# Attention and expert kernel on one core: slot work spread over units, scatters and gathers issued by step

## The chip, the core and the metric

The kernel runs on one core of a Trainium2 chip. The metric is the device time of one execution in microseconds (us); lower is better. PE is the matrix engine (PEld its weight loads), DVE the vector engine, ACT the scalar engine, POOL GpSimd, and SP the engine that only issues DMAs and waits. The profile gives TensorE's granted clock as a share of full speed: 1.00 is 2.4 GHz and 0.50 is 1.2 GHz, the two levels between which it moves.

## What is computed

```python
xn = layernorm(x)                                   # x: (4, 1024, 128), fp32
q, k, v = xn @ Wq.T, xn @ Wk.T, xn @ Wv.T           # 16 heads of 8, rope on q and k
attn = softmax(causal(q @ k.T / sqrt(8))) @ v @ Wo.T
probs = softmax(xn @ router_w.T)                    # 4096 tokens, 8 experts
top_w, top_idx = top_k(probs, 2);  top_w /= sum(top_w) + 1e-9
ffn = sum over the 2 chosen of top_w * (relu(xn @ w1[e].T + b1[e]) @ w2[e].T + b2[e])
out = x + attn + ffn
```

## The kernel before

**Layout of the work.** There are four phases. A prologue normalises the rows, projects q, k and v with rope for the four sequences, writes the split parts of q and k to HBM (`parts_d`) and makes the router's logits. Then come 16 *units* (4 sequences x 4 groups of 4 heads). After the first two steps of unit 12 the *experts* run: 72 tiles of 128 slots each. Then the rest of unit 12 and units 13, 14 and 15, and the end: scaling, output projection and stores. `LAST` is 12.

**A unit has 12 steps**, one for each block of 128 keys in a half of 512 queries: steps 0 to 3 for the first half, steps 4 to 11 for the second. PE makes the scores of the step two further on (line 1271, `LEAD` is 2), ACT turns them into `probs` (line 764), POOL masks the diagonal block (line 660, steps 0 to 3 and 8 to 11), and PE multiplies with the values (line 1306). Beside it PE makes *items*, score pieces for later units (line 1237), and DVE takes their row maxima (lines 882 and 874). At step 6 DVE splits the next unit's maxima (lines 966 to 975), PE turns them (line 1260), at step 7 (`TURN`) DVE copies them to `mrow` (line 991), and SP stores them into the next unit's stack with four DMAs (line 418), for which the next unit's scores wait. `heads_out` (line 997) copies a half's result at steps 3 and 11. POOL's `stage_v` (line 649) prepares the next unit's values at step 3, which makes it a good mark of a unit's length.

**The slots.** Each token goes to two experts. DVE picks them (lines 930 to 947), PE counts tokens by two matmuls (`count_tokens`), and DVE works out each token's slots (`slot`, lines 1098 to 1118), which expert each tile belongs to (`expert`, lines 1121 to 1124) and the gates (lines 949 to 957). Each of these DVE steps waits for the one before. POOL *scatters* the normalised rows into `slots_in_d` in units 0 to 11 (line 634, 64 indirect DMAs) and *gathers* the experts' results from `slots_out_d` in units 12 to 15 (line 643, 64 indirect DMAs into 8 buffers, `GOT`); DVE adds each gathered block in `combine` (line 1029), and gather n waits for combine n - 8. The tables `SCATTERS` and `TRANSFERS` say how many POOL issues after each of a unit's 8 diagonal steps, `COMBINES` how many DVE adds at each of the 12 steps.

**What sets the order.** Each engine has one program, in the order written, and semaphores between engines; nothing is scheduled by a tool. `keep_warm` (line 1159) issues matmuls whose result nobody reads. POOL's part before unit 0 and before the rest of unit 12:

```python
            pool.wait_ge(s["slots_zeroed"], 16 * 4)
            pool.wait_ge(s["routed"], 1)
            pool.wait_ge(s["xn_ready"], B)
            all_units(pool, unit, None, before_last)   # before_last: waits for all 72 result stores
```

Since POOL does not take part in the experts, `before_last` stands ahead of unit 12's first mask.

Of the kernel before, what the change touches and what calls it, by code (L numbers as in the profile page):

```python
# [5 lines left out]
F32 = mybir.dt.float32  # L6
# [7 lines left out]
P = 128  # L14
# [11 lines left out]
PARTS = 2  # L26
# [96 lines left out]
def block_program(nc, x, w_projs, router, w_experts, b2, rope_t, consts, masks, out,  # L123
                  parts_d, zero_rows_d, heads_d, slots_in_d, slots_out_d, sums_d):
    ctx = ExitStack()
    with ctx:
# [51 lines left out]
        below = xnT[:, 0:TILES * E].rearrange("p (j e) -> p j e", e=E)  # L178
        ends = xnT[:, TILES * E:TILES * (E + 1)]
# [77 lines left out]
        zeros_ready slots_zeroed scattered """  # L257
# [57 lines left out]
        WARM = [30, 45, 1, 10, 22, 6]  # L315
# [7 lines left out]
        INVERTS = {4: 0, 5: 1, 7: 2}  # L323
# [6 lines left out]
        COMBINES = [[0, 0, 1, 0, 1, 2, 3, 3, 2, 1, 1, 1], [0, 1, 1, 0, 2, 2, 3, 3, 2, 1, 1, 1],  # L330
                    [0, 1, 1, 0, 2, 3, 3, 3, 2, 1, 1, 1], [1, 1, 1, 0, 1, 2, 2, 2, 2, 1, 1, 0]]
# [23 lines left out]
        def _(sp):  # L355
# [56 lines left out]
            def store_max_rows(u, par):  # L412

                sp.wait_ge(s["scores_read"], (u + 1) * MI)
                for g in range(2):
# [14 lines left out]
            def unit(u, r):  # L430
# [24 lines left out]
                if isinstance(u, int) and u == LAST + 3:  # L455
# [4 lines left out]
                    return  # L460
                store_heads(u, 1)
# [112 lines left out]
            store_max_rows(0, 0)  # L574
# [8 lines left out]
        def _(pool):  # L583
# [47 lines left out]
            def scatter(n):  # L631

                k2, t = divmod(n, NT)
                pool.indirect_dma_start(out=slots_in_d, out_offset=bass.IndirectOffsetOnAxis(  # L634
# [3 lines left out]
            def gather(n):  # L638

                t, k2 = gather_order(n)  # L640
                if n >= GOT:
# [11 lines left out]
            def unit(u, r):  # L653
                for n, (c, kb, q0) in enumerate(STEPS):
                    if kb >= 4 * c:
# [7 lines left out]
                        d = c * 4 + kb - 4 * c  # L663
                        if d == 3 and more(u, 1):
# [4 lines left out]
                        if u < LAST:  # L669
                            for i in share_of(SCATTERS, u, d):  # L670
                                scatter(i)
                        else:
                            for i in share_of(TRANSFERS, r, d):
                                gather(i)
# [7 lines left out]
            pool.wait_ge(s["slots_zeroed"], 16 * 4)  # L682
            pool.wait_ge(s["routed"], 1)
            pool.wait_ge(s["xn_ready"], B)
            all_units(pool, unit, None, before_last)
# [3 lines left out]
        def _(act):  # L689
# [104 lines left out]
            def experts():  # L794
                act.wait_ge(s["experts_loaded"], 16 * E)
                stage_w1(0, 0)
# [3 lines left out]
            for written in parts_written:  # L800
                act.wait_ge(written[1], 16 * PARTS * 2)
            unit(0)
# [11 lines left out]
        def _(dve):  # L814
# [134 lines left out]
            step(v.scalar_tensor_tensor(r_s[:, 0, :], share[:, 0, :], 1e-9, share[:, 1, :], ALU.add, ALU.add))  # L949
            step(v.reciprocal(r_s[:, 1, :], r_s[:, 0, :]))  # L950
            step(v.tensor_tensor(share[:], share[:], r_s[:, 1, :].unsqueeze(1).broadcast_to([P, 2, NT]), ALU.mult))
            step(v.tensor_tensor(gates[:], one1, wide(share[:, 0, :]), ALU.mult))
            step(v.tensor_tensor(m1, one2, wide(share[:, 1, :]), ALU.mult))
            v.tensor_tensor(gates[:], gates[:], m1, ALU.add).then_inc(s["chosen_ready"], 1)
            dve.wait_ge(s["logits_made"], B)
            dve.wait_ge(s["gT_made"], 1)
            v.tensor_copy(gT.rearrange("p a b -> p (a b)"), bank[:, 2, 0:2 * P]).then_inc(s["gT_kept"], 1)

# [40 lines left out]
            def unit(u, r):  # L999
                for j in range(NS):  # L1000
# [7 lines left out]
                    if j == TURN and more(u, 1):  # L1008
                        copy_rows(u + 1, (r + 1) % 4)
                    if isinstance(u, int) and u == UNITS - 1 and j == 6:  # L1010
# [71 lines left out]
            def experts():  # L1082
                dve.wait_ge(s["experts_loaded"], 16 * E)
                stage_w2(0, 0, expert_of(0))
                all_tiles(dve, tile)
                copy_y(TILES - 1, (TILES - 1) % 4)

            for n in range(sum(PREPARED.values()), NI):
# [5 lines left out]
            et = "p (e t) -> p e t"  # L1094
            earlier = bank[:, 3, 0:NT * E].rearrange("p (t e) -> p t e", e=E)
            inblock = bank[:, 3, NT * E:2 * NT * E].rearrange("p (t e) -> p e t", e=E)
            dve.wait_ge(s["counted"], 1)
            step(v.tensor_copy(total.rearrange(et, e=E), inblock))

            step(v.tensor_tensor_scan(upto, inner, total, 0.0, ALU.mult, ALU.add))  # L1100
            count = upto.rearrange(et, e=E)[:, :, NT - 1:NT].rearrange("p e o -> p (e o)")
            step(v.tensor_scalar(r_i[:, 0, :], count, float(ROUND - 1), None, ALU.add))
            bits = ROUND.bit_length() - 1
            step(v.tensor_scalar(r_i[:, 1, :], r_i[:, 0, :], bits, bits, ALU.logical_shift_right,
                                 ALU.logical_shift_left))
# [418 lines left out]
```

## Time and profile before

| | us |
|---|---|
| median of 3 runs | 768.5 (759.3 to 769.29) |
| the profiled execution | 764.56 |
| its span, first to last instruction | 762.8 |
| PE / DVE / ACT / POOL busy | 696.3 / 582.2 / 444.4 / 254.8 |
| mean granted clock | 0.955 |

The span begins at 0. The prologue ends at 107, units 0 to 11 and two steps of unit 12 end at 458, the experts run from 461 to 603, and the rest follows. PE counts as busy for 91% of the span, but its busy time includes stretches in which its matmuls take up to twice as long at the lower clock. Ends of matmuls are modelled, and a waiting engine is put down to what released it last; "remote" and "issue" mean that the trace names no releaser.

### The profile page before, as it was taken

The numbers are of one execution on the slowest core, as the hardware profiler recorded it, in microseconds if no ns is written. First come the engines' busy times: TensorE is split into PE (matmuls) and PEld (weight loads), VectorE is DVE, ScalarE is ACT, GpSimd is POOL, SyncE is SP. The second block draws the span as 40 slices with busy tenths as digits, with TensorE's granted clock in tenths as the row PEclk, the third lists the DMA queues.
The fourth block names the chain that finished last, engine by engine and source line by source line (L and its number), as shares of the span: only waits on it lengthen the run. The fifth ranks groups of instructions, "written<-read, shape, count | busy, mean of one in ns | idle before, by whom it ended". The sixth has DMA issues, their size and how long they took to land. (4 is left out here: it accounts for less than half of the span.)

```text
span 762.8 us, 18457 instructions
## 1 busy us (share of the span) xinstructions
PE 696.3 (91%) x6064; PEld 398.4 (52%) x6064; DVE 582.2 (76%) x1337; ACT 444.4 (58%) x962; POOL 254.8 (33%) x308
## 2 busy tenths in 40 slices
PE   8799898999999999999999997999999779788887
PEld 3456343434434444444444447999999624343434
DVE  6956978879879889889889884666666559797344
ACT  3455024666666677677677675666666346556541
POOL 2556212424334333433523520000000146565821
PEclk9999998999999999999999998999999869898989
DMA  8499950236355255134225413222222521111654
GB/s 222 129 231 231 236 100 20 45 78 102 73 116 100 60 96 80 38 54 79 50 45 77 63 32 95 78 69 69 69 69 69 135 52 38 46 34 40 162 126 130
DMA packets 64621, 69.36 MB, mean 91 GB/s; under 512 B 9934, under 2 KB 52430, under 8 KB 64490
## 3 DMA queue, kind: packets, MB, share of 16 engines
q1 hardware_dynamic: 60458, 60.08, 36.2%
q0 software_dynamic: 4096, 8.40, 4.2%
q8 instruction: 40, 0.66, 0.4%
q14 instruction: 27, 0.22, 0.1%
HBM read 41.11 MB, written 26.67 MB: 89 GB/s over the span
## 5 line engine op out<-in xcount | busy, mean ns | idle before, releaser
L764 ACT ACTIVATE probs<-bank 128x512 f32<-128x512 f32 (+2 forms) x640 | 314.8, 555 | 214.0 <-PE bank L1271 185.1
L882 DVE TENSOR_REDUCE mx<-bank 128x2 f32<-128x1024 f32 (+2 forms) x200 | 220.6, 1130 | 51.1 <-PE bank L1245 33.8
L1271 PE MATMUL bank<-stack 64*128 64x512 f32 (+3 forms) x768 | 196.4, 439 | 25.8 <-issue 16.0
L660 POOL TENSOR_SCALAR_AFFINE_SELECT probs<-probs 128x512 f32<-128x512 f32 x128 | 81.1, 635 | 406.7 <-ACT probs L764 253.6
L1306 PE MATMUL bank<-probs,vst 128*32 128x256 f32 (+2 forms) x2560 | 199.6, 387 | 5.0 <-POOL probs L660 5.0
L1271 PEld LDWEIGHTS bank<-stack 64*128 64x128 f32 x768 | 89.9, 189 | 157.5 <-issue 77.7
L1237 PE MATMUL bank<-stack 64*128 64x512 f32 (+3 forms) x768 | 149.2, 382 | 6.1 <-DVE mx L882 4.0
L874 DVE CUSTOM_DVE_ANT_0 q_high<-bank,later_s 128x384 bf16<-128x384 f32 (+1 forms) x240 | 135.1, 619 | 9.5 <-PE bank L1237 8.0
L1306 PEld LDWEIGHTS bank<-probs,vst 128*32 128x32 f32 x2560 | 52.2, 110 | 88.9 <-issue 72.7
L1237 PEld LDWEIGHTS bank<-stack 64*128 64x128 f32 x768 | 78.0, 193 | 39.1 <-issue 19.6
L1355 PE MATMUL bank<-tiles_s,staged 128*128 128x128 f32 x576 | 78.3, 280 | 0.7 <-ACT tiles_s L768 0.7
L1373 PE MATMUL bank<-staged,q_high 128*128 128x128 f32 x576 | 76.2, 275 | 0.5 <-DVE k_high L1062 0.5
L643 POOL DMA_INDIRECT k_high<-slots_out_d,slot x64 | 61.3, 958 | 40.6 <-DVE xn_all L1029 27.3
L1355 PEld LDWEIGHTS bank<-tiles_s,staged 128*128 128x128 f32 x576 | 71.4, 195 | 1.4 <-ACT tiles_s L768 1.4
L1373 PEld LDWEIGHTS bank<-staged,q_high 128*128 128x128 f32 x576 | 70.0, 192 | 0.7 <-issue 0.6
L778 ACT COPY staged<-early 128x516 f32 x72 | 44.8, 622 | 42.8 <-DVE q_high L1071 41.4
L634 POOL DMA_INDIRECT slots_in_d<-xn_all,slot x64 | 62.6, 977 | 12.8 <-issue 12.8
L1071 DVE TENSOR_SCALAR q_high<-bank,staged 128x128 f32<-128x128 f32 x144 | 43.9, 346 | 23.7 <-PE bank L1355 20.4
L789 ACT ACTIVATE q_high<-bank,staged 128x128 f32<-128x128 f32 x144 | 44.6, 360 | 1.6 <-PE bank L1373 1.1
L1062 DVE COPY k_high<-bank 128x128 f32<-128x128 f32 x72 | 21.0, 292 | 27.7 <-PE bank L1373 27.7
L997 DVE COPY xnT<-bank 128x512 f32<-128x512 f32 x32 | 22.0, 687 | 17.4 <-remote 10.3
L1159 PE MATMUL bank<-ones_b 128*128 128x512 bf16 x122 | 32.1, 415 | 1.1 <-POOL ones_b L586 1.1
(137 smaller groups left out, 477.4 us busy)
## 6 DMA issues: line engine op xcount, KB each, us to landing
stack<-parts_d SPq DMA_DIRECT2D x96, 128.0 KB
slots_in_d<-const_s SPq DMA_DIRECT2D x4, 1152.0 KB, 10.5
tiles_s<-slots_in_d SPq DMA_DIRECT2D x72, 64.0 KB, 1.8
slots_out_d<-k_high SPq DMA_DIRECT2D x72, 64.0 KB, 1.6
early<-in_w_experts SPq DMA_DIRECT2D x8, 514.0 KB
stack<-parts_d SPq DMA_DIRECT2D x64, 64.0 KB
parts_d<-probs SPq DMA_DIRECT2D x8, 512.0 KB, 6.1
heads_d<-xnT SPq DMA_DIRECT2D x124, 18.0 KB
```

What stands on the lines that cost most here:

```text
L634: pool.indirect_dma_start(out=slots_in_d, out_offset=bass.IndirectOffsetOnAxis(ap=slot[:, k2, t:t + 1], axis=0), in_=xn_all[:, t, :], in_o ...
L643: pool.indirect_dma_start(out=got[n % GOT], out_offset=None, in_=slots_out_d, in_offset=bass.IndirectOffsetOnAxis(ap=slot[:, k2, t:t + 1], ...
L660: pool.affine_select(out=t, in_=t, compare_op=ALU.is_ge, fill=0.0, base=0, pattern=[[0, HG], [1, P]], channel_multiplier=-1).then_inc(s["d ...
L764: nc.scalar.activation(to, src, ACT.Exp, scale=SCALE).then_inc(s["probs_made"], 1)
L778: nc.scalar.copy(w_s[r % 2][:, 0:F + FC], early[:, bass.ds(e * WIDE, F + FC)]).then_inc(s["w1_staged"], 1)
L874: last = v.tensor_tensor_reduce(hidden_scores[n % 2 * 2 + g][:, 0:w], ms[(r * MI + n) % 2][:, g * HALF:g * HALF + w], later_s[:, HALF - w: ...
L882: v.tensor_reduce(to, src.rearrange("p g (a k) -> p g a k", k=w), AX_X, ALU.max, negate=True).then_inc(s["scores_read"], 1)
L1237: last = mm(at[:, col:col + w], qstk[r][g][:, hp, qb * P:(qb + 1) * P], kstk[r][g][:, hp, c * HALF:c * HALF + w], start=not both or i == 0 ...
L1271: made = mm(st_of(u, n, i)[:, col:col + HALF - q0], kstk[r][g][:, hp, kb * P:(kb + 1) * P], qstk[r][g][:, hp, c * HALF + q0:(c + 1) * HALF ...
L1306: last = mm(pv[32 * h:32 * h + 32, begin:end], vst[r % 2][:, kb, h, :], probs[n % 3][:, h, begin:end], start=kb == 0 and begin == 0, stop= ...
L1355: last = mm(at[:, col:col + P], w_s[r % 2][:, f * P:(f + 1) * P], xtT[r % 2], start=True, stop=True)
L1373: last = mm(pv[:, 0:C], hid[r % 2][:, f * P:(f + 1) * P], w_s[r % 2][:, F + FC + f * C:F + FC + (f + 1) * C], start=f == 0, stop=f == FC - 1)
```

## The change

The slot chain of the prologue is cut up: only the two counts are copied out of PSUM there, and the rest runs on DVE in units 0 to 3 at the end of steps 7, 8 and 9 (`rank`). The gates are made in unit 2 and turned by PE at the start of the experts. POOL issues scatters and gathers by a table with one entry for each of 12 steps, and waits at steps without a mask for that step's `probs`; scatters start in unit 2. The wait for the result stores moves to the first gather (step 3 of unit 12). SP loads the first four expert tiles in unit 11. ACT issues two of the four stores of the first unit's maxima. `keep_warm` calls are shortened before and added between the first scores and ahead of the experts. The inversions of the head sums in unit 13 move from steps 4, 5 and 7 to 8, 9 and 10.

```diff
-        WARM = [30, 45, 1, 10, 22, 6]
+        WARM = [30, 35, 1, 10, 12, 6]
-        INVERTS = {4: 0, 5: 1, 7: 2}
+        INVERTS = {8: 0, 9: 1, 10: 2}
-        SCATTERS = [[1, 0, 0, 3, 1, 0, 0, 1]] * 4 + [[1, 0, 0, 2, 1, 0, 0, 1]] * 8
+        SCATTERS = ([[0] * 12] * 2 + [[0, 0, 0, 1, 1, 1, 1, 1, 1, 0, 0, 1]] * 4 + [[0, 0, 0, 1, 1, 1, 1, 1, 0, 0, 0, 1]] * 5
+                    + [[0, 0, 1, 1, 1, 1, 1, 1, 0, 0, 0, 0]])
-        TRANSFERS = [[1, 0, 0, 11, 2, 1, 0, 2]] * 2 + [[1, 0, 0, 12, 2, 1, 0, 2]] + [[1, 0, 0, 9, 2, 0, 0, 0]]
+        TRANSFERS = [[0, 0, 0, 2, 2, 2, 2, 2, 2, 1, 1, 2], [1, 0, 0, 2, 2, 2, 2, 2, 2, 1, 1, 2],
+                     [1, 0, 0, 2, 2, 2, 2, 2, 2, 1, 1, 2], [1, 1, 1, 2, 2, 2, 2, 2, 1, 0, 0, 0]]
...
 # SP, in unit(u, r), after the maxima of the next unit are stored
+                if isinstance(u, int) and u == LAST - 1:
+                    sp.wait_ge(s["scattered"], 16 * 2 * NT)
+                    for j in range(4):
+                        load_tile(j, j)
                 store_heads(u, 1)
             def experts():
-                sp.wait_ge(s["scattered"], 16 * 2 * NT)
-                for j in range(4):
-                    load_tile(j, j)
                 all_tiles(sp, tile)
...
-            store_max_rows(0, 0)
+            store_max_rows(0, 0, range(1))
...
 # POOL
             def gather(n):
+                if n == 0:
+                    for r in range(4):
+                        pool.wait_ge(y_stored[r], 16 * TILES // 4)
...
+                    else:
+                        pool.wait_ge(s["probs_made"], banks_before(u, n + 1))
+                    if u < LAST:
+                        for i in share_of(SCATTERS, u, n):
+                            scatter(i)
+                    else:
+                        for i in share_of(TRANSFERS, r, n):
+                            gather(i)
-            def before_last():
-                for r in range(4):
-                    pool.wait_ge(y_stored[r], 16 * TILES // 4)
...
 # ACT, before unit 0
+            act.wait_ge(s["scores_read"], MI)
+            for n in range(2):
+                act.dma_start(qstk[0][1][KROWS + n:KROWS + n + 1, :, :] ..., mrow[0] ...).then_inc(mrow_stored[0], 16)
...
 # DVE: the gates (lines 949 to 957) leave the prologue; the slot chain becomes these functions, called in unit(u, r)
+            v.tensor_copy(place, earlier).then_inc(s["counts_kept"], 1)
+            v.tensor_copy(total.rearrange(et, e=E), inblock).then_inc(s["counts_kept"], 1)
+            def rank(u, j):
+                if (u, j) == (0, TURN):
+                    first_slots()        # was lines 1100 to 1106
+                if (u, j) == (0, TURN + 1):
+                    next_slots()         # 1107 to 1109
+                if (u, j) == (0, TURN + 2):
+                    places()             # 1110 to 1114
+                if (u, j) == (1, TURN):
+                    slots_of(0)          # 1116 to 1118
+                if (u, j) == (1, TURN + 2):
+                    slots_of(1)          # the same, then "routed"
+                if (u, j) == (2, TURN):
+                    share_out()          # 949 to 951
+                if (u, j) == (2, TURN + 2):
+                    gates_out()          # 952 to 954
+                if (u, j) == (3, TURN):
+                    expert_tiles()       # 1121
+                if (u, j) == (3, TURN + 2):
+                    expert_ends()        # 1123, 1124, then "expert_known"
 # DVE, in experts(), after stage_w2
+                dve.wait_ge(s["gT_made"], 1)
+                v.tensor_copy(gT ..., bank[:, 2, 0:2 * P]).then_inc(s["gT_kept"], 1)
...
 # PE
             pe.wait_ge(mrow_stored[0], mrow_count(0, 0))
-            pe.wait_ge(s["gT_kept"], 1)
+            pe.wait_ge(s["scores_read"], MI + AT_START)
             for n in range(LEAD):
                 for h in range(HG):
                     score(0, 0, n, h)
+                    if n or h:
+                        keep_warm(1, 7)
-            pe.wait_ge(s["routed"], 1)
+            pe.wait_ge(s["counts_kept"], 2)
...
                 turn_tile(0, 0)
+                turn_gates()             # waits for probs of unit 12, steps 0 and 1; two transposes
+                keep_warm(3, 7)
                 all_tiles(pe, tile)
```

DVE at the end of the prologue, from the copy of the first unit's maxima to the first maxima of unit 1's items. Before:

```order
L991 COPY mrow<-bank 64x128
L1098 COPY staged<-bank 128x256
L1100 SCALAR_TENSOR_TENSOR staged<-const_s,staged 128x256
L1102 TENSOR_SCALAR r_i<-staged 128x8
L1104 TENSOR_SCALAR r_i<-r_i 128x8
L1106 CAST r_e<-r_i 128x8
L1107 MEMSET r_e 128x8
L1108 SCALAR_TENSOR_TENSOR r_e<-r_e 128x8
L1109 TENSOR_TENSOR r_e<-r_e 128x8
L1110 TENSOR_TENSOR staged<-staged 128x256
L1111 TENSOR_TENSOR staged<-staged,r_e 128x256
L1114 TENSOR_TENSOR staged<-bank,staged 128x256
```

Nine more rows follow (lines 1116 to 1124) before the maxima of line 882. Now, where line 893 is the old 882 and 992 the old 991:

```order
L967 TENSOR_TENSOR mx<-mx 128x4x4
L972 CAST mneg<-mx 128x16 x2
L976 TENSOR_TENSOR mneg<-mx,mneg 128x16 x2
L992 COPY mrow<-bank 64x128
L1104 COPY staged<-bank 128x256
L1105 COPY staged<-bank 128x256
L893 TENSOR_REDUCE mx<-bank 128x2x2 x4
```

Two copies stand where 21 instructions stood; the rest is in units 0 to 3.

POOL from step 8 of unit 11 into unit 12, with what each waits for. Before:

```order
L634 DMA slots_in_d<-xn_all,slot 9216x128
L660 AFFINE_SELECT probs<-probs 128x4x128 [waits y_stored3,probs_made,y_stored2,y_stored0,y_stored1]
L643 DMA k_high<-slots_out_d,slot 128x128
L660 AFFINE_SELECT probs<-probs 128x4x128 [waits probs_made] x3
L649 COPY vst<-v_all 128x32x8 [waits probs_used]
L643 DMA k_high<-slots_out_d,slot 128x128 x7
L643 DMA k_high<-slots_out_d,slot 128x128 [waits combined] x4
```

Now (line 670 is the old 660, 659 the old 649, 653 the old 643):

```order
L670 AFFINE_SELECT probs<-probs 128x4x128 [waits probs_made] x8
L659 COPY vst<-v_all 128x32x8 [waits probs_used]
L653 DMA k_high<-slots_out_d,slot 128x128 [waits y_stored2,y_stored3,y_stored1,y_stored0]
L653 DMA k_high<-slots_out_d,slot 128x128
L653 DMA k_high<-slots_out_d,slot 128x128 [waits probs_made]
...
L653 DMA k_high<-slots_out_d,slot 128x128 [waits combined,probs_made]
L653 DMA k_high<-slots_out_d,slot 128x128 [waits combined]
```

The wait for the result stores stands behind unit 12's first four masks, and every second gather waits for the `probs` of its step.

PE at the start of the experts. Before:

```order
L1271 MATMUL bank<-stack 128x384 x2
L1237 MATMUL bank<-stack 128x384 x2
L1364 MATMUL bank<-const_s,tiles_s 128x128
L1355 MATMUL bank<-tiles_s,staged 128x128 x4
```

Now (1423 is the old 1364, 1414 the old 1355, 1278 the turning of the gates, 1214 `keep_warm`):

```order
L1330 MATMUL bank<-stack 128x384 x2
L1296 MATMUL bank<-stack 128x384 x2
L1423 MATMUL bank<-const_s,tiles_s 128x128
L1278 MATMUL bank<-const_s,logits 128x128 x2
L1214 MATMUL bank<-ones_b 128x512 x3
L1414 MATMUL bank<-tiles_s,staged 128x128 x4
```

The gates are turned between the first tile's turn and its first product.

## Rows read from the trace of the kernel before

**Rows 1.** Windows over chosen stretches: busy us of each engine, granted clock, DMA

```profile
core 0: us, PE busy (x) PEld busy (x) DVE busy (x) ACT busy (x) POOL busy (x), PEclk, DMA share, GB/s
151.20:240.40 89.20, 83.25 (x823) 37.20 (x819) 74.05 (x157) 59.05 (x120) 33.70 (x47) 0.96 0.46 89
268.00:295.70 27.70, 26.83 (x280) 12.15 (x273) 24.62 (x53) 19.64 (x40) 10.27 (x15) 1.00 0.44 74
612.10:650.10 38.00, 32.16 (x279) 13.66 (x283) 29.06 (x68) 19.69 (x40) 21.69 (x28) 0.86 0.19 44
650.10:685.90 35.80, 29.41 (x278) 13.16 (x281) 31.48 (x75) 20.12 (x40) 21.71 (x28) 0.90 0.15 39
685.90:719.00 33.10, 27.07 (x237) 11.75 (x237) 20.50 (x46) 19.90 (x40) 22.08 (x27) 0.90 0.31 76
```

**Rows 2.** Timeline, end of the prologue: start, length, engine, line, names [idle before]

```profile
85.91 0.42 DVE L947 TENSOR_TENSOR staged<-staged 128x256 bf16<-128x256 f32 x1
88.52 0.44 PE L1219 MATMUL bank<-const_s,logits 128*128 128x128 f32 x2 [0.46 <-DVE logits L954]
89.60 10.27 DVE L882 TENSOR_REDUCE mx<-bank 128x2 f32<-128x1024 f32 x9
101.46 2.50 SPq L418 DMA_DIRECT2D stack<-mrow  x4
101.98 4.92 PE L1159 MATMUL bank<-ones_b 128*128 128x512 bf16 x22
106.83 0.73 PE L1271 MATMUL bank<-stack 64*128 64x512 f32 x3
109.46 0.69 DVE L882 TENSOR_REDUCE mx<-bank 128x4 f32<-128x512 f32 x1 [0.25 <-DVE expert L1124]
```

**Rows 3.** Windows: steps 0 to 3 of units 0 and 1, and of unit 12

```profile
112.20:122.60 10.40, 10.40 (x72) 4.31 (x71) 7.38 (x21) 3.05 (x8) 4.79 (x7) 0.58 0.22 45
138.90:145.70 6.80, 6.61 (x85) 3.27 (x82) 5.49 (x11) 3.67 (x9) 2.25 (x3) 1.00 0.06 17
605.60:615.80 10.20, 8.62 (x56) 3.06 (x58) 5.07 (x15) 1.75 (x4) 6.32 (x9) 0.50 0.73 111
```

**Rows 4.** Timeline, start and end of the experts

```profile
461.03 0.45 PE L1364 MATMUL bank<-const_s,tiles_s 128*128 128x128 f32 x1 [3.49 <-DMA tiles_s<-slots_in_d]
461.83 2.08 PE L1355 MATMUL bank<-tiles_s,staged 128*128 128x128 f32 x8 [0.35 <-ACT tiles_s L768]
468.90 1.06 PE L1355 MATMUL bank<-tiles_s,staged 128*128 128x128 f32 x8
606.41 0.62 POOL L660 TENSOR_SCALAR_AFFINE_SELECT probs<-probs 128x512 f32<-128x512 f32 x1 [151.98 <-DMA slots_out_d<-k_high]
607.18 1.08 PE L1306 MATMUL bank<-probs,vst 128*32 128x256 f32 x8 [3.21 <-POOL probs L660]
```

**Rows 5.** Timeline, POOL's run of eight gathers in unit 12, ACT and PE beside it

```profile
612.67 0.98 POOL L643 DMA_INDIRECT k_high<-slots_out_d,slot  x1 [0.16 <-issue]
...
621.29 1.08 ACT L764 ACTIVATE probs<-bank 128x512 f32<-128x512 f32 x2 [3.03 <-remote]
621.45 0.94 POOL L643 DMA_INDIRECT k_high<-slots_out_d,slot  x1 [0.30 <-issue]
621.94 0.49 PE L1271 MATMUL bank<-stack 64*128 64x512 f32 x1 [3.13 <-issue]
```

**Rows 6.** The same view: ACT in unit 15's run of gathers, the last of four

```profile
729.91 1.09 ACT L764 ACTIVATE probs<-bank 128x512 f32<-128x512 f32 x2 [3.14 <-remote]
```

**Rows 7.** Lines view, unit 13: DVE's adds and inversions, mean ns

```profile
L1029 DVE SCALAR_TENSOR_TENSOR xn_all<-k_high,share,xn_all 128x128 f32<-128x128 f32 x17 | 6.0, 383 | 0.0
L1035 DVE RECIPROCAL tiles_s<-tiles_s 128x128 f32<-128x128 f32 x3 | 2.8, 943 | 0.0
```

**Rows 8.** Timeline, the last gathers and the add that waits

```profile
743.87 0.94 POOL L643 DMA_INDIRECT k_high<-slots_out_d,slot  x1 [0.15 <-issue]
750.64 0.35 DVE L1029 SCALAR_TENSOR_TENSOR xn_all<-k_high,share,xn_all 128x128 f32<-128x128 f32 x1 [8.00 <-DMA k_high<-slots_out_d,slot]
```

More of the change, by code:

```diff
@@ L177, in block_program @@
         rt2 = [staged[:, 1, i * NT * E:(i + 1) * NT * E] for i in range(4)]
-        below = xnT[:, 0:TILES * E].rearrange("p (j e) -> p j e", e=E)
-        ends = xnT[:, TILES * E:TILES * (E + 1)]
+        below = staged[:, 0, 0:TILES * E].rearrange("p (j e) -> p j e", e=E)
+        ends = staged[:, 0, TILES * E:TILES * (E + 1)]
         gates = logits
@@ L410, in load_stacks, with store_max_rows @@
                                  ).then_inc(stack_loaded[r], 16)
-            def store_max_rows(u, par):
+            def store_max_rows(u, par, halves=range(2)):
                 sp.wait_ge(s["scores_read"], (u + 1) * MI)
-                for g in range(2):
+                for g in halves:
                     for n in range(2):
@@ L662, in unit @@
                                            ).then_inc(s["diag_masked"], 1)
-                        d = c * 4 + kb - 4 * c
-                        if d == 3 and more(u, 1):
+                        if n == 3 and more(u, 1):
                             if past(u):
@@ new lines, in next_slots, with places @@
+            def next_slots():
+                step(v.memset(r_e[:, 3, :], 1.0))
+                step(v.tensor_tensor_scan(r_e[:, 1, :], r_e[:, 3, :], r_e[:, 0, :], 0.0, ALU.mult, ALU.add))
+                step(v.tensor_tensor(r_e[:, 2, :], r_e[:, 1, :], r_e[:, 0, :], ALU.subtract))
+            def places():
+                step(v.tensor_tensor(upto, upto, total, ALU.subtract))
+                step(v.tensor_tensor(upto.rearrange(et, e=E), upto.rearrange(et, e=E),
+                                     r_e[:, 2, :].unsqueeze(2).broadcast_to([P, E, NT]), ALU.add))
+                step(v.tensor_tensor(place, place, upto.rearrange("p (e t) -> p t e", e=E), ALU.add))
@@ L1117, in _, with slots_of @@
+            def slots_of(n):
+                step(v.tensor_tensor(m0, (one1, one2)[n], place, ALU.mult))
                 step(v.reduce_sum(r_s[:, n, :], m0, AX_X))
                 step(v.tensor_copy(slot[:, n, :], r_s[:, n, :]))
-            dve.wait_ge(s["v_made"], B)
-            step(v.tensor_tensor(below, r_e[:, 1, :].unsqueeze(1).broadcast_to([P, TILES, E]),
-                                 starts.unsqueeze(2).broadcast_to([P, TILES, E]), ALU.is_le))
-            step(v.reduce_sum(ends, below, AX_X))
@@ L1124, in _, with share_out @@
-            step(v.tensor_scalar(expert[:], ends, float(E - 1), None, ALU.min))
-            dve.sem_inc(s["routed"], 1)
-            dve.wait_ge(parts_written[0][0], 16 * PARTS * 2)
-            dve.wait_ge(s["later_ready"], 1)
+                if n:
+                    dve.sem_inc(s["routed"], 1)
+            def share_out():
+                step(v.scalar_tensor_tensor(r_s[:, 2, :], share[:, 0, :], 1e-9, share[:, 1, :], ALU.add, ALU.add))
+                step(v.reciprocal(r_s[:, 3, :], r_s[:, 2, :]))
+                step(v.tensor_tensor(share[:], share[:], r_s[:, 3, :].unsqueeze(1).broadcast_to([P, 2, NT]), ALU.mult))
@@ new lines, in gates_out, with expert_tiles @@
+            def gates_out():
+                step(v.tensor_tensor(gates[:], one1, wide(share[:, 0, :]), ALU.mult))
+                step(v.tensor_tensor(m1, one2, wide(share[:, 1, :]), ALU.mult))
+                v.tensor_tensor(gates[:], gates[:], m1, ALU.add).then_inc(s["chosen_ready"], 1)
+            def expert_tiles():
+                dve.wait_ge(s["chosen_ready"], 2)
+                step(v.tensor_tensor(below, r_e[:, 1, :].unsqueeze(1).broadcast_to([P, TILES, E]),
+                                     starts.unsqueeze(2).broadcast_to([P, TILES, E]), ALU.is_le))
@@ new lines, in expert_ends @@
+            def expert_ends():
+                step(v.reduce_sum(ends, below, AX_X))
+                step(v.tensor_scalar(expert[:], ends, float(E - 1), None, ALU.min))
+                dve.sem_inc(s["expert_known"], 1)
+            def rank(u, j):
[17 more added lines that the diff above has]
+                    expert_ends()
```

69 lines of the change are left out of this document (29 added, 40 removed).

## The prediction

> **What bounds the kernel now.** I read the windows by stage first, with one unit to a row, because the busy shares of the whole span mix stages with different limits. A unit in the middle of the run takes 27.7 us, in which PE is busy for 26.8 and DVE for 24.6, at a full clock: PE bounds it, and DVE has 3.1 us to spare [rows 1]. Units 1 to 3, from one `stage_v` to the next, take 89.2 us together, 6.1 more than three times 27.7, with the same busy DVE and ACT and a clock of 0.96. What differs there is POOL: its table lets it issue three scatters in a row, where later units have two. Units 12, 13 and 14 take 38.0, 35.8 and 33.1 at clocks of 0.86 and 0.90, with DVE busy for 29.1, 31.5 and 20.5 and PE for 27.1 in the third [rows 1]. So no engine is full there; 19.3 us are waiting (106.9 less 29.1, 31.5 and 27.1).
>
> Then I read the timeline at the places where a stretch is longer than its engines' work. At the end of the prologue the first scores, at 106.83, stand behind 22 warming matmuls, which stand behind nothing but the engine's own order, while the maxima are stored by four DMAs of SP [rows 2]. Steps 0 to 3 of unit 0 and of unit 12 take 10.4 and 10.2 us at clocks of 0.58 and 0.50; the same steps of unit 1 take 6.8 at 1.00 [rows 3]. The experts begin after 3.49 us of an idle PE and end with 3.21 [rows 4]. In a run of eight gathers ACT and PE are idle for 3.03 and 3.13 us at the same moment, with no releaser in the trace; the last of four such places shows 3.14 [rows 5, 6].
>
> **The change part by part.** The sum is made against the profiled execution, 764.56, which lies 3.9 below the median of 768.5.
>
> *First scores, −4.3.* DVE's picked experts are ready at 86.33, and its first maximum starts at 89.60, behind the gates and the transposes of PE at 88.52 [rows 2]. Without both, and with ten warming matmuls fewer (0.22 each, 4.92 by 22), PE counts at 86.4 (two matmuls, 0.4), makes the first pieces, and DVE reads them 0.7 after: 87.45, 2.15 sooner. The rest of the chain moves along, and SP begins the stores at 99.3. Two stores on SP take 1.25 of the 2.50 for four; ACT issues the others beside it. Twelve warming matmuls take 2.7 and end at 102.5 instead of 106.90, and the scores start there, if the stores have landed: −4.3. The trace bounds the landing: the four stores had ended issuing at 103.96 and PE went on at 106.83, so at most 2.9 later. That gives 103.5 at worst, −3.3.
>
> *Head of unit 0, −2.5.* It takes 3.6 more than that of unit 1 [rows 3]. Two things go: DVE, busy with the slot chain until 109.2, reads unit 1's pieces again at 109.46 [rows 2], and PE idles or waits in between; now the chain is two copies, and PE is kept active by warming matmuls between the first scores. Both ends are open: nothing returns if the clock falls all the same (0), all of it if not (3.6). I take two thirds.
>
> *Units 1 to 3, −6.1, and the moved work, +1.* Scatters now come one to a step, from unit 2 on. The trace has no such spacing; the nearest row is the unit with two in a row, 27.7. The moved chain lies between 101.5 and 109.2, 7.7 us [rows 2], and the gates add 2.15: some 9.8 us of DVE in four units, at steps 7 to 9, where DVE's queue also holds the maxima copied for the next unit. Four times the 3.1 us of spare DVE are 12.4, so that cover is there, and I take 1 for what falls at a bad moment. If the cover were gone, all 9.8 would show. Unit 0 and unit 1 have no scatters at all; that they must catch up later costs nothing by count, since no unit issues more than seven where it was six.
>
> *Start of the experts, −3.* PE's 3.49 us go if the tiles lie there already [rows 4]. Behind them the first tile's products took 2.08 us instead of 1.06, at the lower clock; with the next tile's that is at most some 1.5 more, if PE is not idle long enough to lose its clock. Against it stand two transposes (0.44), three warming matmuls (0.7) and ACT's and DVE's staging of the weights, which is next late: PE had been idle for about as long as they worked. Bounds −1.5 and −4.5, value −3. What SP does in unit 11 (a wait for the 64 scatters, the last at step 7, ahead of the loads and the head stores) sits at the end of that unit, and nothing waits on SP there before unit 12.
>
> *End of the experts, −6.* The mask at 606.41 waited for the last result stores, and PE for the mask: 3.21 [rows 4]. With the wait behind unit 12's four masks, 3.1 goes. The head of unit 12 then ran 3.4 us longer than at full clock [rows 3]; if PE does not idle, most of this goes too: −2.9. The bounds are −3.1 and −6.5.
>
> *Gathers in units 12 to 14, −7.* The 19.3 us of waiting, less 1.3 that lie in the head of unit 12 after its `stage_v` and are counted there, leave 18.0. Some of it is the run of eight to twelve gathers at one step. The change spaces them, but not far: two at each of steps 3 to 8, each 1.25 us from start to start [rows 5], are 2.5 us of issuing in a step of 2.3 us (27.7 by 12). POOL still issues nearly back to back through half of the unit. Moreover DVE's adds, 0.38 each, and the three inversions of 0.94 [rows 7] stay, with unit 13 bound by DVE at 31.5. All of it would be −18, none of it 0; I take −7, nearer to none, because the row nearest to the new spacing is the run itself.
>
> *Unit 15 and the end, −0.5.* DVE's add at 750.64 came 6.8 us after the gather at 743.87 was issued, and it was idle for 8.00 us [rows 8]; the last gather is still at step 8.
>
> Sum: −4.3 −2.5 −6.1 +1 −3 −6 −7 −0.5 = −28.4, so 736.2 for an execution like the profiled one, and with half of its distance to the median **738**.
>
> **The rivals.** *The gathers cost what they cost, spaced or not: 745.* The idle places at the runs [rows 5, 6] are brief beside 18 us, and the lower clock of these units may come from PE's share in them. Then the −7 is 0. For it: the nearly unbroken issuing. Against: units with two scatters in a row show none of it.
> The Trainium skill bears on this (SBUF — State Buffer, "SBUF: two separate sides"): PE, ACT and DVE's own pair of ports never wait on anyone, and engine ports and DMA ports are disjoint. By that rule the spacing changes nothing and the time is that of this rival; but rows 5 show PE and ACT idle together at a run of gathers, so the trace does not quite agree.
>
> *The stalls vanish: 727.* If the 3 us places and the clock both come from runs longer than two, the term is −18 and the time 11 less than forecast.
>
> *New waits eat it: 758.* Adds now follow their gathers by one step. A loaded gather took 6.8 us [rows 8], three steps; eight buffers hold the queue, but if DVE waits 0.5 us at each of the 24 steps with two adds, that is 12 us, and an uncovered slot chain adds 8: 738 + 20.
> For an unloaded gather the Trainium skill (DMA: Bandwidth & Descriptors, "Anatomy of one DMA — SWDGE (gpsimd) path") gives about 2.0 us and the bytes over 436e3; my estimate from it is 2.15 for 64 KB, within a step, and by it this rival costs nothing. The 6.8 of the trace is measured with other traffic.
>
> *Slower than before: 785.* The clock stays at its lower level in units 12 to 15, because PE waits a little at every step instead of much at one. Its price is the ratio of the heads, 10.4 to 6.8, or 1.53 [rows 3], on the stretch that now takes about 140: four units of 42 are 169, +29. With 12 us of waits this is 41, and the 7 of the gathers are not gained: 738 + 48, about 785. [...]
>
> **How the numbers follow.** The forecast, 738 with its own bounds from 729 to 748, gets 0.55; spacing without effect 0.18; the vanished stalls 0.12; new waits 0.10; slower 0.05. That the change does not do what it says is small and inside these. The range must leave out no more than 2 in 10: from 722, below the case at 727, to 758, that of the new waits. Two per cent of 768.5 is 15.4, about what a measurement of this kernel can tell from no change; the limits are 753.1 and 783.9. The forecast, both cases of the gathers and a little of the new waits lie below 753: 0.83 faster, 0.13 same, 0.04 slower.
>
> **What would show it.** First scores near 102.5; steps 0 to 3 of unit 0 in 7 to 8 us at full clock; units 1 to 3 at 28 each, with the slot work in DVE's idle places; PE idle below 1 us at the start of the experts, and none before the first product of unit 12; units 12 to 14 at 34, 34 and 30. I am wrong if PE still shows places of 3 us beside spaced gathers, if DVE waits for `k_high` at the steps after, or if the clock in units 1 to 3 stays below 1.00 without runs of scatters.

## The result, and the profile after

The changed kernel takes 744.8 us (median of four runs, 741.8 to 749.1) against 768.9 (759.3 to 769.4). The ratio is 0.972, with a 95% interval from 0.964 to 0.980: faster. The forecast was 738, with a range of 722 to 758. The profiled execution has a span of 740.8 us, 22.0 less than the one before, and a mean granted clock of 0.965.

The windows over the stretches that [rows 1] shows for the kernel before, then unit 13's values staged to the end as one stretch, and the first probabilities to the values of unit 2:

```profile
core 0: us, PE busy (x) PEld busy (x) DVE busy (x) ACT busy (x) POOL busy (x), PEclk, DMA share, GB/s
149.10:233.90 84.80, 80.95 (x823) 36.89 (x819) 78.05 (x172) 58.76 (x120) 31.05 (x43) 1.00 0.49 89
261.70:289.30 27.60, 26.73 (x277) 12.17 (x273) 24.54 (x53) 19.60 (x40) 12.19 (x18) 1.00 0.43 80
596.80:629.00 32.20, 29.81 (x275) 13.18 (x273) 27.75 (x66) 19.91 (x40) 22.18 (x27) 0.89 0.35 65
629.00:667.30 38.30, 32.48 (x273) 13.88 (x265) 32.01 (x76) 19.60 (x40) 21.77 (x28) 0.84 0.15 38
596.80:740.80 144.00, 125.05 (x1027) 58.28 (x1023) 101.60 (x212) 73.14 (x148) 82.64 (x96) 0.89 0.36 86
105.20:149.10 43.90, 40.92 (x356) 17.99 (x356) 35.57 (x87) 25.59 (x52) 8.55 (x14) 0.92 0.20 31
```

The three units that had runs of three scatters now take 84.8 where they took 89.2, at a clock of 1.00 instead of 0.96. The middle unit is as it was. The unit after the first gathers takes 32.2 instead of 38.0, but the next one 38.3 instead of 35.8. The same two long stretches before read so:

```profile
612.10:762.80 150.70, 123.18 (x1033) 57.25 (x1033) 100.72 (x212) 73.84 (x148) 79.29 (x95) 0.90 0.31 78
107.40:151.20 43.80, 39.84 (x349) 18.05 (x348) 35.96 (x83) 25.04 (x52) 14.96 (x21) 0.88 0.24 41
```

PE's idle time in the long last stretch is the length less its busy time: 27.5 before, 19.0 now. The clock there did not rise. The stretch from the first probabilities to the values of unit 2 kept its length, 43.8 and 43.9. Inside it something did move. Here is what follows the start of PE's product of step 3 of unit 0, before and then in the changed kernel:

```profile
122.60:151.20 28.60, 25.32 (x262) 11.49 (x261) 25.57 (x57) 17.52 (x37) 7.98 (x12) 1.00 0.13 28
```

```profile
117.72:149.10 31.38, 28.75 (x262) 12.52 (x261) 28.55 (x67) 17.63 (x37) 5.65 (x9) 0.89 0.09 18
```

The timeline at the end of the prologue, which answers to [rows 2]:

```profile
88.04 0.42 DVE L958 TENSOR_TENSOR staged<-staged 128x256 bf16<-128x256 f32 x1
89.63 10.28 DVE L893 TENSOR_REDUCE mx<-bank 128x2 f32<-128x1024 f32 x9 [1.17 <-PE bank L1312]
101.49 1.21 SPq L420 DMA_DIRECT2D stack<-mrow  x2
101.51 1.47 ACTq L810 DMA_DIRECT2D stack<-mrow  x2
101.99 1.27 DVE L893 TENSOR_REDUCE mx<-bank 128x4 f32<-128x512 f32 x2
102.01 2.76 PE L1214 MATMUL bank<-ones_b 128*128 128x512 bf16 x12
104.70 0.49 PE L1330 MATMUL bank<-stack 64*128 64x512 f32 x2
```

The pick of the experts (first row) ends at 88.46, 2.1 later than before. No edit reaches that part, and in the twelve kernels below, which leave it as it is in the changed one, the pick ends between 85.7 and 87.2. In this execution PE's clock was at its lower level for 10.2 us up to 51 instead of 3.4, so the 2.1 are a matter of the execution. From the pick on, the first maximum comes after 1.17 us instead of 3.27, and the first scores after 16.2 instead of 20.5.

The start of the experts and their end, which answer to [rows 4]:

```profile
451.54 0.33 PE L1423 MATMUL bank<-const_s,tiles_s 128*128 128x128 f32 x1 [1.14 <-DVE mx L885]
451.71 0.38 PE L1278 MATMUL bank<-const_s,logits 128*128 128x128 f32 x2
451.92 0.81 PE L1214 MATMUL bank<-ones_b 128*128 128x512 bf16 x3
452.57 1.05 PE L1414 MATMUL bank<-tiles_s,staged 128*128 128x128 f32 x8
...
592.67 0.50 PE L1330 MATMUL bank<-stack 64*128 64x256 f32 x4 [0.43 <-issue]
593.27 0.64 PE L1365 MATMUL bank<-probs,vst 128*32 128x256 f32 x8
```

PE is idle for 1.14 us instead of 3.49, now behind DVE's last maximum, the next in line; and its first products run at full clock (1.05 for eight). At the end the 3.21 us ahead of the first product of unit 12 are gone.

The gathers of unit 13, in the same view as [rows 5]:

```profile
633.39 0.95 POOL L653 DMA_INDIRECT k_high<-slots_out_d,slot  x1 [1.51 <-ACT probs L768]
...
637.14 0.95 POOL L653 DMA_INDIRECT k_high<-slots_out_d,slot  x1 [0.30 <-issue]
...
639.64 0.94 POOL L653 DMA_INDIRECT k_high<-slots_out_d,slot  x1 [0.30 <-DVE xn_all L1032]
640.57 1.08 ACT L768 ACTIVATE probs<-bank 128x512 f32<-128x512 f32 x2 [3.06 <-remote]
641.22 0.79 PE L1330 MATMUL bank<-stack 64*128 64x512 f32 x1 [2.38 <-ACT probs L768]
```

The table asks for two at a step, but POOL still issues six in a row (633.39 to 639.64), since two take 2.5 us and the steps are about as long. ACT is idle for 3.06 us beside them, as before.

### The profile page after: what moved, and what is told of

Read it like the earlier page. It is cut to its first block and busy times, and to the rows that moved or that the text cites. A ratio compares the mean times of both kernels' runs of the same rounds, so it can differ in the third digit from the quotient of the medians.

```text
span 740.8 us, 18461 instructions
## 1 busy us (share of the span) xinstructions
PE 692.5 (93%) x6054; PEld 396.7 (54%) x6054; DVE 581.4 (78%) x1338; ACT 444.1 (60%) x962; POOL 258.8 (35%) x308
## 5 line engine op out<-in xcount | busy, mean ns | idle before, releaser
L670 POOL TENSOR_SCALAR_AFFINE_SELECT probs<-probs 128x512 f32<-128x512 f32 x128 | 84.4, 659 | 342.5 <-ACT probs L768 341.4
L1365 PE MATMUL bank<-probs,vst 128*32 128x256 f32 (+2 forms) x2560 | 196.5, 382 | 2.9 <-DVE xnT L998 1.5
L1365 PEld LDWEIGHTS bank<-probs,vst 128*32 128x32 f32 x2560 | 52.2, 109 | 85.7 <-issue 68.2
L1414 PE MATMUL bank<-tiles_s,staged 128*128 128x128 f32 x576 | 76.8, 276 | 0.4 <-ACT tiles_s L772 0.4
L1074 DVE TENSOR_SCALAR q_high<-bank,staged 128x128 f32<-128x128 f32 x144 | 43.9, 346 | 19.3 <-PE bank L1414 15.9
L1032 DVE SCALAR_TENSOR_TENSOR xn_all<-k_high,share,xn_all 128x128 f32<-128x128 f32 x64 | 23.1, 395 | 14.4 <-DMA k_high<-slots_out_d,slot 13.6
```

Of the source, the lines that this page charges most:

```text
L670: pool.affine_select(out=t, in_=t, compare_op=ALU.is_ge, fill=0.0, base=0, pattern=[[0, HG], [1, P]], channel_multiplier=-1).then_inc(s["d ...
L1365: last = mm(pv[32 * h:32 * h + 32, begin:end], vst[r % 2][:, kb, h, :], probs[n % 3][:, h, begin:end], start=kb == 0 and begin == 0, stop= ...
L1414: last = mm(at[:, col:col + P], w_s[r % 2][:, f * P:(f + 1) * P], xtT[r % 2], start=True, stop=True)
```

## The experiments

Each group of kernels ran on one chip with runs of the kernel before. Its median was 768.9, 767.4, 771.0 and 769.0 in the four groups, so ratios are compared. One more reading is used below: stages by landmarks of the profiles. From unit 4's values to unit 12's, kernels with equal code agree to 0.2 us (221.4 to 221.6 us in ten of them, 221.9 in an eleventh); the clock does not fall there. Where it does they agree less. The changed kernel and seven others have the same code up to the values of unit 2, and from the first probabilities to there they take 43.0 or 43.1 us (five), 43.8 (two) and 44.2; after unit 12 the differences are larger still.

**gathers_bunched** gives POOL its runs of nine to twelve back:

```diff
-TRANSFERS = [[0,0,0,2,2,2,2,2,2,1,1,2], [1,0,0,2,2,2,2,2,2,1,1,2], ...
+TRANSFERS = [[0,0,0,12,0,0,0,0,2,1,0,2], [1,0,0,11,0,0,0,0,2,1,0,2], ...
+COMBINES = [[0,0,0,0,2,2,3,3,2,1,1,1], ...
```

> The changed kernel with the gathers alone put back to one run of 9 to 12 at step 3 and the adds to match. Run-length theory (an unbroken run of six or more gathers makes the signals of PE late by about 3 us and then costs clock): from unit 12's values being staged to the end of the span it takes 150 us again, as before the change, instead of 144.0, so about 751; idle places of 3 us on ACT and PE in all four units. Count theory (64 gathers cost the same in any spacing): the stretch stays within 2 us of 144 and the time at 745.

751.2 us, ratio 0.985 (0.973 to 0.997); the last stretch is 155.4.

**gathers_spread** spreads them further:

```diff
+TRANSFERS = [[0,0,0,2,1,2,1,2,1,2,1,2], [1,1,1,1,2,1,2,1,2,1,2,2],
+             [1,1,1,1,2,1,2,1,2,1,2,2], [2,1,1,2,2,2,2,2,2,0,0,0]]
+COMBINES = the same, two steps later
```

> The changed kernel with the gathers spread further: one at most steps, two at every second, adds two steps behind. Run-length theory: POOL's longest unbroken run is 4, no idle place of 3 us on ACT is left in units 13 and 14, their periods fall from 32.2 and 38.2 to about 31 each, and the time to 737 to 740. Count theory: 745, with the same 3 us places at other moments.

740.3 us, ratio 0.972 (0.963 to 0.981); the last stretch is 139.2.

**gathers_left_out:**

```diff
 def gather(n):
+    if n >= GOT: return
```

> The changed kernel with 56 of the 64 gathers left out, so that the adds take old buffers and the experts' part of the output is wrong; waits and adds stay. It gives the floor: from unit 12's values staged to the end 144.0 us now. If gathers still cost what lies above the work of the engines, this falls to 125 to 130, and the time to 727 to 731. If the clock and the waits there come from the adds, the inversions and PE's own share, it stays above 138 and the time above 739.

730.5 us, ratio 0.958 (0.950 to 0.965); 134.0.

**adds_later** has the gathers of the changed kernel and adds two steps behind, to separate the two edits of the spread version.

> The gathers as in the changed kernel, two at steps 3 to 8, but the adds two steps behind instead of one. If spacing the gathers was what the spread version gained, this one stays with the changed kernel, 745 to 748, from unit 13's values to the end 144 to 149. If the later adds gained it, that stretch is 139 to 141 and the time 740.

749.6 us, ratio 0.975 (0.969 to 0.981); 151.0. Windows of the last stretch, in the order bunched, spread, left out, adds later:

```profile
596.10:751.50 155.40, 133.44 (x1027) 61.06 (x1023) 102.93 (x212) 73.44 (x148) 82.03 (x96) 0.82 0.32 79
```

```profile
595.60:734.80 139.20, 120.05 (x1027) 56.68 (x1023) 101.52 (x212) 72.48 (x148) 83.17 (x96) 0.93 0.36 88
```

```profile
594.60:728.60 134.00, 117.34 (x1027) 55.80 (x1023) 98.87 (x212) 72.77 (x148) 27.38 (x40) 0.93 0.27 64
```

```profile
598.40:749.40 151.00, 129.01 (x1027) 59.58 (x1023) 101.64 (x212) 72.80 (x148) 82.79 (x96) 0.87 0.33 82
```

PE's idle time (length less busy) is 22.0, 19.1, 16.7 and 22.0, against 27.5 before and 19.0 in the changed kernel. Its busy time follows the clock column, 133 us at 0.82 and 117 at 0.93, for the same 1027 matmul rows. The scale for all of these is what kernels with equal tables show. The changed kernel and seven below have its tables of gathers and adds, and their last stretch takes 143.9 to 149.6 us, with 18.2 to 21.6 us of idle PE.

The bunched kernel's 155.4 lies 5.8 above the longest of them, which speaks for a cost of bunching and against the count theory's "within 2 us of 144". It is no proof: the idle time of 22.0 is hardly outside their range, the kernel with spaced gathers and later adds shows the same 22.0 and 151.0, and the intervals of the two ratios, 0.973 to 0.997 and 0.964 to 0.980, overlap. Nor is the spacing the whole of what went from PE's idle time: with runs as long as before it is 22.0, not 27.5. So of the 8.5 us that went, putting the runs back returned 3.0. The other 5.5 have a cause that no run isolates; the inversions of unit 13, which also moved, were not put back.

Without gathers 2.3 us less are idle than in the changed kernel and PE is busy for 7.7 less, at a clock of 0.93 instead of 0.89. What the gathers still cost in this pair, 10.0 us, is mostly lower clock. That spreading further helps is not shown: the ratios 0.972 and 0.972 are equal, and 139.2 stands alone. The floor of 134.0 lies between what the two views expected, 125 to 130 and over 138. The later adds gained nothing by themselves.

The 3 us places come with gathers, but not with a long run. In the last stretch ACT has five idle places above 2.5 us that the trace puts down to "remote" before the change, two in the changed kernel, one each with the gathers bunched and spread, four with the later adds, and none without gathers. The bunched kernel issued seven in a row in unit 13 and showed shorter waits:

```profile
633.00 0.97 POOL L657 DMA_INDIRECT k_high<-slots_out_d,slot  x1 [0.16 <-issue]
...
640.52 0.94 POOL L657 DMA_INDIRECT k_high<-slots_out_d,slot  x1 [0.30 <-issue]
...
643.12 2.07 ACT L772 ACTIVATE probs<-bank 128x512 f32<-128x512 f32 x4 [1.76 <-remote]
```

**scatters_bunched:**

```diff
+SCATTERS = ([[0] * 12] * 2 + [[1,0,0,3,0,0,0,0,1,1,0,1]] * 4 + [[1,0,0,3,0,0,0,0,1,0,0,1]] * 6)
```

> The changed kernel with scatters three in a row at step 3 in units 2 to 11. If the run of three is what cost units 1 to 3 their 2 us, ten units now take 1 to 2.5 us more each: periods of 29 to 30 instead of 27.6 to 28.2, some lower clock, and 755 to 765. If what units 1 to 3 gained came from something else, periods stay at 28 and the time at 745.

762.1 us, ratio 0.991 (0.984 to 0.999). Windows from unit 4's values staged to unit 12's, here and in the changed kernel:

```profile
206.00:443.40 237.40, 221.77 (x2190) 99.72 (x2184) 201.37 (x420) 157.64 (x320) 93.79 (x124) 0.96 0.38 69
```

```profile
205.70:427.20 221.50, 214.42 (x2188) 97.51 (x2184) 197.69 (x420) 156.77 (x320) 94.42 (x125) 1.00 0.41 74
```

Runs of three cost 15.9 us in eight units, 2 in each on average: 7.4 as slower matmuls (clock 0.96) and 8.5 as PE's idle time. In seven of the eight units PE has one idle place of about 1 us (0.94 to 1.06), 5.5 us after the values are staged, behind ACT; in the changed kernel no unit there has one above 0.6. The first of them:

```profile
211.53 0.49 PE L1329 MATMUL bank<-stack 64*128 64x512 f32 x1 [0.94 <-ACT probs L767]
```

This is the cleanest result of the study, at the same count of scatters, and the only one of these kernels whose ratio has an interval clear of the changed kernel's.

**gates_back** puts lines 949 to 957 and the two transposes back ahead of the first maxima:

```diff
 v.tensor_tensor(chosen_b, ...).then_inc(s["chosen_ready"], 1)
+step(...)  # the six gate instructions
+dve.wait_ge(s["gT_made"], 1)
+v.tensor_copy(gT..., bank[:, 2, 0:2 * P]).then_inc(s["gT_kept"], 1)
```

> The changed kernel with the gates and their transposes back ahead of the first maxima. If the gates were on the path, the first scores come 2.2 us later after the pick of the experts than in the changed kernel (16.2 us from the start of the pick's last instruction, now 16.66 including its wait, becomes about 18.8) and the time rises by 2 to 747. Rival: the warming matmuls and the landing of the stores set the first scores anyway, and nothing moves.

751.4 us, ratio 0.977 (0.968 to 0.987). DVE's timeline of this kernel:

```profile
86.66 0.42 DVE L958 TENSOR_TENSOR staged<-staged 128x256 bf16<-128x256 f32 x1
...
89.81 0.42 DVE L968 COPY tiles_s<-bank 128x256 f32<-128x256 f32 x1 [0.60 <-PE bank L1277]
90.35 2.36 DVE L893 TENSOR_REDUCE mx<-bank 128x2 f32<-128x1024 f32 x2
```

From the pick to the first maximum it is 3.27 us again, not 1.17: 2.1 us are the gates. The first probabilities come 20.15 us after the pick instead of 16.8. This kernel had a stretch at half clock on the way (90.7 to 100.9), and two kernels without this edit had one as well (gathers_bunched and adds_later, 18.4 and 19.6). So the 2.1 are shown at the first maximum, and what they are worth at the first scores is not seen by itself.

**chain_back** calls `first_slots`, `next_slots`, `places` and `slots_of` behind the copies of the counts.

> The changed kernel with the slot chain of units 0 and 1 (16 instructions, 5.8 us) back behind the copies of the counts. My theory: in unit 0 DVE is full (31.9 of 34.8 us), so moving the chain there bought nothing: the sum from the first scores to the values of unit 2 staged (44.4 us before and after) stays within 1 us, and the time stays at 745. Rival, the forecast's: DVE late at unit 1's pieces let the clock fall; then steps 0 to 3 of unit 0 go back to 10 us and the time rises by 2.5 or more.

754.7 us, ratio 0.979 (0.971 to 0.986). PE's timeline shows what went wrong with this edit:

```profile
100.09 2.76 PE L1209 MATMUL bank<-ones_b 128*128 128x512 bf16 x12
107.43 0.55 PE L1325 MATMUL bank<-stack 64*128 64x512 f32 x2 [4.58 <-DVE mx L893]
```

The first scores now wait for DVE's reading of unit 1's pieces (the wait that protects the bank of the new warming matmuls), and DVE stands behind the chain. PE is idle for 4.58 us, then at half clock for 17.1 us. That is the price of the pair, not of the chain, so two more kernels took it apart.

**unwarmed_scores** drops the warming matmuls between the first scores, and that wait; **old_start** is that with the chain back:

```diff
-pe.wait_ge(s["scores_read"], MI + AT_START)
-        if n or h: keep_warm(1, 7)
```

> The changed kernel without the warming matmuls between the first scores and without the wait that protects their bank. If they kept the clock up, the half clock comes back in steps 0 to 3 of unit 0 as it was before (10 us instead of 7) but no longer later in the unit: 43.5 us from the first probabilities to the values of unit 2 stay within 1, since in either case one such stretch falls in it. Forecast's view: 2.5 us longer.

> The same, and the slot chain of units 0 and 1 back behind the counts. The earlier kernel with the chain there also made the first scores wait for it, through that bank's wait; here they do not. If the chain itself costs: the 43.5 us become 46 or more. If only the wait cost: first scores 16.8 after the pick, 43.5 again, and the 2.3 us that units 2 and 3 gained without the chain stay: 743.

744.9 us, ratio 0.969 (0.962 to 0.976), and 743.9, ratio 0.967 (0.961 to 0.974). Windows from the first probabilities to the values of unit 2:

```profile
103.00:147.00 44.00, 40.30 (x349) 17.82 (x348) 35.49 (x87) 25.08 (x52) 8.44 (x13) 0.88 0.21 31
```

```profile
104.00:147.60 43.60, 40.30 (x349) 17.77 (x348) 36.94 (x86) 25.11 (x52) 7.94 (x14) 0.88 0.22 32
```

43.8 before, 43.9 changed, 44.0 and 43.6 here, where kernels with the changed kernel's own start show 43.0 to 44.2: the place of the chain and the warming matmuls moved nothing that can be seen in unit 0. With the chain back, the next two units took 55.7 us instead of 56.6. So my view, that moving the chain bought nothing, holds by old_start, and the rise of chain_back was the wait.

**loads_back** puts SP's wait and the four tile loads back into `experts()`.

> The changed kernel with the four tile loads back at the start of the experts. If the loads were worth the 3.6 us that went there, PE is idle again for about 3.4 us ahead of the first tile's turn and the experts start 3 us later, 748. Rival: with the gates turned by PE there, DVE and ACT are late as well and only 1 us returns.

747.7 us, ratio 0.967 (0.959 to 0.976). In PE's timeline:

```profile
452.60 0.45 PE L1422 MATMUL bank<-const_s,tiles_s 128*128 128x128 f32 x1 [3.49 <-DMA tiles_s<-slots_in_d]
...
454.55 1.59 PE L1413 MATMUL bank<-tiles_s,staged 128*128 128x128 f32 x8
```

From unit 12's values to the product of the eleventh tile it is 48.6 us instead of 45.2. The 3.4 are seen in the stage (2.35 more of idle PE, and the clock at its lower level from 452.2 to 455.7, where the changed kernel kept it up); the timed runs, with their intervals of a per cent, cannot show them.

**wait_back** puts `before_last` back.

> The changed kernel with the wait for the result stores back ahead of unit 12's first mask. PE is idle for 3.2 us at the first product of unit 12; 4.6 us went between the last tile and the values of unit 13. If the idle place also set the clock, all of the 4.6 returns and the time is 749; if the clock falls anyway (it did, at 603.5), 3.1 returns: 748.

750.7 us, ratio 0.973 (0.967 to 0.980). POOL and PE in its timeline:

```profile
592.71 1.81 POOL L670 TENSOR_SCALAR_AFFINE_SELECT probs<-probs 128x512 f32<-128x512 f32 x3 [147.48 <-ACT probs L772]
```

```profile
593.49 1.08 PE L1369 MATMUL bank<-probs,vst 128*32 128x256 f32 x8 [1.90 <-POOL probs L670]
594.50 0.80 PE L1300 MATMUL bank<-stack 64*128 64x512 f32 x2
```

From the last tile's product to the values of unit 13 it is 10.8 us instead of 7.4 (12.0 before). The idle place itself is only 1.90; the rest is the clock, which fell at 592.5 here, so that eight products take 1.08 us, not 0.64. In the changed kernel it fell at 603.5.

**spread_later** has the tables of gathers_spread and all of `rank` one unit later, with scatters from unit 3.

> The spread gathers (two adds behind) together with the slot chain, gates and tile tables one unit later, in units 1 to 4, scatters from unit 3. Spreading theory as measured: 740. If DVE being full in unit 0 is what made that unit long, first scores to the values of unit 2 fall from 43.5 to 42 or less and unit 4 pays 0.6 for it: 739. Rival: unit 0 is long through its clock and its own pieces, 43 stays, 740 to 741.

745.3 us, ratio 0.970 (0.964 to 0.975). The first stretch is 43.0 again, and the last one 145.6, with the tables that gave 139.2. So the 139.2 was in part a lucky clock, and this is no better version. None of the eleven kernels that do the whole work is clearly faster than the changed one.

## Why the prediction came out as it did

The sum was for an execution like the profiled one: −28.4 forecast, −22.0 measured. By its own steps, with the first landmark of each stage from [rows 2, 4] and the profiles above:

| step | forecast | measured |
|---|---|---|
| the prologue up to the pick, untouched | 0 | +2.1 |
| first scores | −4.3 | −4.3 |
| head of unit 0 | −2.5 | +0.1 |
| units 1 to 3, with the moved work | −5.1 | −4.4 |
| units 4 to 11 | 0 | −0.5 |
| start of the experts | −3 | −3.6 |
| end of the experts, head of unit 12 | −6 | −4.6 |
| gathers, unit 15 | −7.5 | −6.7 |

*First scores* held to the tenth, with some luck: of the nine kernels with this start seven show it, and two, in which the clock fell on the way, were 1.6 and 2.9 us later. 2.1 are the gates, which gates_back shows at the first maximum; the other 2.2, for the shorter warming and the divided stores, are what remains and were not taken apart. *Units 1 to 3* held, and scatters_bunched shows that the run of three is the cause. The row is not sharp, since a stretch of lower clock can fall on either side of the mark at unit 2's values: five of the kernels with this code show 43.0 or 43.1 and 86.2 or 86.3 us for the two rows, where the changed kernel shows 43.9 and 84.8 and the kernel before 43.8 and 89.2. *The start of the experts* held, with DVE's maximum as the next in line. *The end of the experts* was a little too large: 3.4 of the 4.6 came back with the wait in wait_back, in part as lower clock. The remaining 1.2 are open; PE's idle place there was 1.90, not the 3.21 of before.

*The head of unit 0* is the step that failed. It took the 3.6 us of lower clock in steps 0 to 3 as something that better feeding of PE would give back. For these steps alone this came true: 7.2 us at full clock instead of 10.4, between the marks of [rows 3]. But the stretch at half clock, which had begun at 110.6, now began at 122.2, and the rest up to unit 2's values took 31.4 us at a clock of 0.89 instead of 28.6 at 1.00; the part ahead of unit 0's first product, with the new warming matmuls in it, grew by 0.5. What failed is that the local gain was taken for a gain of the whole. Chain, warming matmuls and their wait were taken out one after the other, and the stretch from the first probabilities to unit 2's values stayed within 43.0 to 44.2 us in all kernels (49.5 only where the first scores had waited for the chain). The case that "the clock falls all the same (0)" was the lower end of that term, and it is the one that came.

*The gathers* gave 6.7 with unit 15, close to the 7.5, but this is in part luck. The last stretch took 144.0 us here, and kernels with the same tables show up to 149.6 (146.9 on average, so 3.8 less than before). The division is another one too: 8.5 us less of idle PE, and the clock no better (0.89 against 0.90). Of the 8.5, only 3.0 came back when the gathers were bunched again. The idle time that the gathers cause, by gathers_left_out, is 2.3 us in the changed kernel and 5.3 in the bunched one, far from the 18 that the windows had offered as waiting of DVE and PE. That the −7 came from the spacing is therefore not shown.

Of the rivals, that the gathers cost the same spaced or not named 745, and 745 was measured; but the time agrees for other reasons (unit 0, the late prologue and the head of unit 12 make up the difference). For scatters spacing did matter: runs of three cost 15.9 us. For gathers the rival is made unlikely by the bunched stretch of 155.4, and is not excluded. The rule that the prediction set beside it, that of the Trainium skill (SBUF — State Buffer, "SBUF: two separate sides"), would leave PE and ACT untouched by POOL's transfers; that rule is about ports, and no run here shows whether ports, signals or the clock carried the cost, only that there is one. New waits did not eat the gain: DVE waits for gathers seven times, 13.6 us in all with 8.27 of it at the end, against five times and 12.9 before. One of the prediction's signs of being wrong did come: ACT still has two places of 3 us beside the gathers, with PE idle for 2.38 at each. The slower case did not come.

The forecast of the lengths of units 12 to 14 ("34, 34 and 30") had the first two at 32.2 and 38.3. Kernels with the same tables differ by 5.7 us in the last stretch. An estimate for one unit at the end of this program is worth no more than that.

## What to carry to other kernels

Where POOL issues indirect DMAs beside matmuls, try pacing them by the other engines' steps, one at a step. For scatters this is shown here; for gathers it is likely. Check in the trace what run is left: a table that says two may still run together. Read a stretch of lower clock as something that moves rather than as something in one place: count its cost only when an experiment makes it go away over a whole unit. And before moving scalar work off an early path, look for the single wait that it stands before; here six instructions of gates and two transposes, ahead of the first maximum, were worth 2.1 us, and the sixteen of the slot chain nothing measurable.

## What the runs showed of the hardware that was not expected

Three scatters in a row, 1.25 us apart, cost PE about 2 us a unit, half as idle time and half as lower clock. Single ones cost no more than two in a row (27.6 us for a unit with six, against 27.6 to 27.7 before); no run leaves scatters out, so that they cost nothing is not shown.

The last gather of the changed kernel, alone in its queue, took 7.41 us from issue to landing:

```profile
721.34 7.41 DMA k_high<-slots_out_d,slot
```

Loads of 256 KB were issued beside it, output stores of 512 KB each followed from 723.35, and DVE waited 8.27 us for it. The eight gathers of gathers_left_out took 2.5 us in the median. For such a transfer the Trainium skill (DMA: Bandwidth & Descriptors, "Anatomy of one DMA — SWDGE (gpsimd) path") leads to an estimate of 2.15 us for 64 KB; the 2.5 is near it, and the 7.41 beside that traffic is far above it.

Kernels whose last 144 to 150 us hold the same instructions differ by up to 5.7 us there, in PE's idle time (18.2 to 21.6) and in how long the clock is at its lower level (28 to 47 us). From unit 4 to unit 12, where the clock does not fall, they agree to 0.2 us in all but one.
